# A graph-transformer layer: the feed-forward's first layer and its gelu move behind the summed messages

## The reference

```python
xn = layernorm(x)
# graph attention, 4 heads of 64
h = (xn @ W).reshape(-1, 4, 64)
e = leaky_relu(a_src[src] + a_dst[dst], 0.2)
ex = exp(e - segment_max(e, dst)[dst])
out = segment_sum(ex / segment_sum(ex, dst)[dst] * h[src], dst)
x = x + sigmoid(out + bias) + mixer(xn)
# mixer: softmax of the keys over all nodes, key-value context, queries, a gelu gate, a projection
# feed-forward
y = layernorm(x)
weights = y @ wr + br
chosen = the nodes with the 3124 largest weights
x = x + y, and for the chosen + (gelu(y @ w1 + b1) @ w2 + b2) * weight
```

## Time and profile before

| | |
|---|---|
| median of 3 runs | 1738.97 us |
| profiled execution | 1737.92 us |
| its span, first to last instruction | 1736.1 us |
| TensorE busy | 1156.1 us, 67% |
| VectorE busy | 1040.8 us, 60% |
| GpSimd busy | 853.7 us, 49% |
| ScalarE busy | 568.8 us, 33% |
| mean granted TensorE clock | 0.831 of 2.4 GHz |
| DMA traffic | 212.01 MB, 122 GB/s |

### The profile page before, as it was taken

One profiled execution on the slowest core, in us unless ns is written; L12 is line 12 of the kernel. 1 busy time (PEld: TensorE's weight loads), 2 busy tenths in 40 slices (PEclk: granted clock), 3 DMA queues, 4 the chain that ended last, 5 costly groups with the idle time before them and its releaser, 6 DMA issues. The chain is left out here.

```text
span 1736.1 us, 26200 instructions
## 1 busy us (share of the span) xinstructions
PE 1156.1 (67%) x6583; PEld 864.7 (50%) x6583; DVE 1040.8 (60%) x2649; ACT 568.8 (33%) x1372; POOL 853.7 (49%) x891
## 2 busy tenths in 40 slices
PE   5985546465667777666767686676676766867871
PEld 4653334343455555455555464554555544645651
DVE  6662344446565666666656666576566566666657
ACT  4442222231333333333333333333342333333540
POOL 0703234534566565565655665655556556556000
PEclk9997667777789879898798888988888889788995
DMA  9245154443454454454454544544545444445204
GB/s 255 78 94 123 48 163 117 122 110 101 124 139 132 125 137 122 124 139 120 127 133 120 136 123 125 134 128 125 138 116 137 119 128 130 127 127 138 55 1 148
DMA packets 165872, 212.01 MB, mean 122 GB/s; under 512 B 49492, under 2 KB 131220, under 8 KB 165672
## 3 DMA queue, kind: packets, MB, share of 16 engines
q0 software_dynamic: 39984, 110.94, 25.4%
q1 hardware_dynamic: 117538, 97.15, 19.6%
q10 hardware_dynamic: 8306, 3.41, 0.9%
HBM read 165.93 MB, written 45.46 MB: 122 GB/s over the span
## 5 line engine op out<-in xcount | busy, mean ns | idle before, releaser
L754 POOL DMA_INDIRECT ring<-feat_d,idx x832 | 815.5, 980 | 659.6 <-issue 470.0
L1696 PE MATMUL bank<-ring,hot 128*64 128x265 f32 x1664 | 318.3, 534 | 284.1 <-issue 201.1
L1696 PEld LDWEIGHTS bank<-ring,hot 128*64 128x64 f32 x1664 | 171.8, 190 | 412.3 <-issue 332.4
L1304 DVE TENSOR_TENSOR ring<-ring,bank 128x1024 f32<-128x1024 f32 x208 | 239.8, 1215 | 1.8 <-ACT bank L1491 1.4
L1724 PE MATMUL bank<-late,w_s 128*128 128x128 f32 x1568 | 213.6, 295 | 8.5 <-ACT late L1531 7.8
L1724 PEld LDWEIGHTS bank<-late,w_s 128*128 128x128 f32 x1568 | 207.9, 210 | 14.3 <-ACT late L1531 8.8
L1675 PE MATMUL bank<-w_s,hT 128*128 128x256 f32 x784 | 191.8, 399 | 3.7 <-ACT hT L1538 3.7
L1491 ACT ACTIVATE bank<-diff 128x64 f32<-128x64 f32 x52 | 11.8, 228 | 476.8 <-DVE diff L1291 317.0
L1675 PEld LDWEIGHTS bank<-w_s,hT 128*128 128x128 f32 x784 | 151.2, 199 | 24.3 <-ACT hT L1538 4.3
L1287 DVE TENSOR_TENSOR ring<-bank,lastT 128x64 f32<-128x64 f32 x52 | 11.7, 225 | 236.2 <-remote 210.6
L1538 ACT ACTIVATE hT<-bank,b_s 128x128 f32<-128x128 f32 x392 | 109.3, 376 | 119.1 <-remote 117.7
(11 more groups left out here) (265 smaller groups left out, 1671.3 us busy)
## 6 DMA issues: line engine op xcount, KB each, us to landing
parts_d<-zero SPq DMA_DIRECT2D x59, 265.0 KB
parts_d<-wout SPq DMA_DIRECT2D x208, 66.2 KB
lists<-dloc_d SPq DMA_DIRECT2D x104, 128.0 KB
ring<-feat_d,idx POOLq DMA_INDIRECT x832
parts<-parts_d SPq DMA_DIRECT2D x49, 265.0 KB
xs<-in_x SPq DMA_DIRECT2D x50, 128.0 KB
big<-in_x SPq DMA_DIRECT2D x7, 896.0 KB, 10.8
out<-xnT SPq DMA_DIRECT2D x7, 896.0 KB, 4.2
```

What stands on the lines that cost most here:

```text
L754: pool.indirect_dma_start(out=ring[:, u * TI + q, 0:AW], out_offset=None, in_=feat_d, in_offset=bass.IndirectOffsetOnAxis(ap=idx[:, u, q:q ...
L1304: V.tensor_tensor(feats, feats, ex[:, g * TG:(g + 1) * TG, :].unsqueeze(3) .to_broadcast([P, TG, HEADS, HD]), ALU.mult).then_inc(S("scaled ...
L1696: mm = T.matmul(bank[2 + n][c * WIN:(c + 1) * WIN, 0:SW], hot[:, q, :], ring[:, u * TI + q, 0:SW], start=(j == 0), stop=(j == TG - 1))
```

## The change

On TensorE `first_ff1` and `other_ff1` are taken out of their places behind the turned scores and behind the projection, and put directly before `ff2`, which is behind the sums and `scores_ahead`. On ScalarE `hidden` is taken out of its place before `keep_sums` and put directly before `inverse_root`. Waits and semaphores are the same.

```diff
-steps(act, [EDGES(exps), MERGE(merge_exp), GELU(hidden), EDGES(keep_sums), LOAD_MIXER(load_mixer), MAXIMUM(first_renorm), CONTEXT(context),
-            SUM(inverse_root), MERGE(gates), SUM(keep_turned)])
+steps(act, [EDGES(exps), MERGE(merge_exp), EDGES(keep_sums), LOAD_MIXER(load_mixer), MAXIMUM(first_renorm), CONTEXT(context),
+            GELU(hidden), SUM(inverse_root), MERGE(gates), SUM(keep_turned)])

-steps(pe, [EDGES(turn_scores), FF1(first_ff1), EDGES(turn_maxima), SUM(project), FF1(other_ff1),
+steps(pe, [EDGES(turn_scores), EDGES(turn_maxima), SUM(project),
            EDGES(first_sums), EDGES(other_sums), AHEAD(scores_ahead), MAXIMUM(maximum), CONTEXT(context), PREPARE(prepare),
-           FF1(ff2),
+           FF1(first_ff1), FF1(other_ff1), FF1(ff2),
            FOLD(fold), MERGE(mixer), SUM(turn_normed), SEARCH(search)])
```

## The result

The changed kernel takes 1924.4 us (median of 4 runs, 1920.2 to 1927.6), the kernel before beside it 1737.9 (1731.0 to 1739.7): 1.108 times, interval 1.104 to 1.112, +186.5 us for a forecast of +212.

A forecast was written before the change was run, and what follows sets the result against it. A chain of waits, no full engine, set 26.7 us a step. With sums' end 20.5 us behind the second gather group, +4.7 a step over 45 steps gave +212 on 1737.9: 1950 us, range 1873 to 2030 (8 in 10: 1780 to 2050).

The forecast's parts named there:

- the forecast's own range: Whole kernel: +3 to +6.5 us a step, 1873 to 2030 us, chance 0.62.
- -0.9 from leaky to the sums: Edge scores' end to summed messages' end: 18.4 us, as the second gather group leads leaky by 2.1 instead of 1.3.
- Put onto the chain, +5.5: Behind the sums: scores, both `ff1` halves, last gelus, handovers and a signal start the inverse root 5.5 us later a step.
- term of 0.7 us for one late signal: Behind the moved `ff1`: allowance for TensorE's signal while gathers run, where signals cost from 0.04 to 5.8 us.
- 5.8 us signal: At the moved `ff1`: 5.8 for 0.7 would add 5.1 us more a step and give 2309 us, kept as an end.
- sums' end = second gather group + 20.5 us: Main loop: this distance stays fixed, so the later group makes the next sums end 4.7 us later a step.
- Faster: Turned maxima to VectorE's start: all 5.8 us of late signal go, -1.2 a step, 1684 us; chance 0.09.
- partial relief: Turned maxima to VectorE's start: half of the 5.8 us late signal goes, +1.7 a step, 1815 us; chance 0.21.
- under 17 us: Leaky to the sums: falling below this, with L1287's remote waits mostly gone, would mean relief; under 13.8 the sign is wrong.
- My argument against them: Leaky to sums: the last step, without gathers, had `ff1` in both old places and took 11.8 us, so gathers matter.
- The signs that were named: If right: L1287 every 31 us, second group 10 to 11 behind sums, L1339 waits about 5 longer, leaky to sums 18 to 19.5.
- "`ff1` or its signal too small": ScalarE waiting over 5 us a step for `ff1` (L1724) would show that this cost was set too low.

The follow-up runs named there:

- e4: The changed kernel with its gathers left out from edge block 6 on, GpSimd writing 4 elements a row instead: 1683.3 us.
- e2: The kernel before with only ScalarE's part of the change (gelu behind the copies of the sums): 1941.3 us against 1743.6, 1.114.
- e6: The kernel before with `ff1`'s products cut to 8 streamed columns, all 128 weight columns kept: 1745.1 us against 1737.8, 1.005.
- e12: The kernel before with `ff1`'s products cut to 8 streamed and 32 weight columns: 1744.6 us against 1742.6, 1.000.
- e5: The kernel before with only TensorE's part of the change (both halves of `ff1` behind the sums): 1889.8 us against 1737.8, 1.086.
- e1: The kernel before with the first half of `ff1` moved behind the projection, directly before the second half: 1787.5 us against 1743.6, 1.026.
- e7: Against the kernel before: `ff1` behind the sums, gelu last on ScalarE, `ff2` of the tile before in the hole ahead of the sums: 1772.8 us, 1.022.
- e8: Like e7, but `ff2` stands directly behind `ff1`, the hole is empty and the gelu is last but one: 1826.8 us against 1737.8, 1.050.
- e9: The kernel of e12 (`ff1` cut to 8 streamed and 32 weight columns) on another chip: 1390.0 us against 1387.7 for the kernel before, 1.001.
- e3: The kernel before with its gathers left out from edge block 6 on, GpSimd writing 4 elements a row instead: 1401.7 us against 1743.6.
- e10: The kernel before with `ff1` in 8 products of 256 columns, on another chip: 1389.8 us against 1387.7, 1.000.
- e11: The kernel before with GpSimd's second gather group waiting for `scores_turned` instead of `ff2_done`, on another chip: 1389.5 us against 1387.7, 0.999.

## Why the prediction came out as it did

- **Sign and size.** 1924 lies in the forecast's own range. But the sum held in part by luck, since two terms missed in opposite directions: +9.1 us instead of +5.5 from the sums to leaky, -5.1 instead of -0.9 from leaky to the sums (cut at ScalarE's copy, +6.5 and -2.5: the same signs, smaller misses). Net +4.0 a step where +4.7 was forecast; 45 x 4.0 = 180 of the 186.5 us.
- **Put onto the chain, +5.5.** The instructions were costed rightly: e4 has +4.6 without any late signal, against 4.8, which is the 5.5 without its 0.7 for the signal. What failed is the term of 0.7 us for one late signal, as all that the gathers could cost there: they cost 4.5 us by the shown ends (16.3 - 11.8), and 1.9 by ScalarE's copy. In the step above TensorE's pause ahead of `ff1` costs 2.8 us (ff1 starts 3.1 behind the sums, not 0.3) and the signal 1.7. The range held a 5.8 us signal at this place as an end without a row near it; the truth lay between.
- **The gathers, "sums' end = second gather group + 20.5 us".** This step failed. The distance is 20.4 to 20.9 in the four kernels with TensorE's old order (before, e2, e6, e12), e2 with its group 4.9 us later behind the sums. It is 14.9 in the changed kernel, 15.4 in e5, 17.2 to 22.2 in e1, e7, e8. Two steps of one trace, both of the same order, could not show this. Nor is the distance constant in that trace: over its 41 steps it is 19.3 to 22.1, so 20.5 and 20.4 agreed by chance. In e9, which has the old order on the other chip, it is 11.8.
- **Faster and partial relief.** Their event happened: the 197.5 us at L1287 went, and leaky to the sums is under 17 us (14.3; to ScalarE's copy 17.1). My argument against them (the step without gathers had `ff1` and took 11.8) showed that gathers are needed for the stall, not that it stays when the chain around it is changed. With 5.1 us gone and 5.5 put on, the step would have grown by 0.4 us and the time by about 1%; it grew by 4.0 since the other side grew by 3.6 more. Their reason, `ff1` around the maxima's turn, fails too: e1 makes L1287 early by taking the first half away, but the sums come no earlier; e12 cuts `ff1`'s work and nothing goes; in e8 L1287 is late with no `ff1` near.
- **The signs that were named.** L1287 recurs every 30.6 us, as forecast. The second group starts 15.7 us behind the sums in the mean, not 10 to 11. VectorE waits 11.4 us a step at L1339 for 3.5 before, 7.9 longer and not 5. ScalarE waits 3.0 us a step ahead of its gelus (118.9 us in 40 steps), so the sign for "`ff1` or its signal too small", over 5 us, did not show, though that term was too small: the rest of the stall stands one place earlier, ahead of the copies of the sums.
- **Not costed.** Taking `ff1` out of the hole lowers the clock of the sums. It costs 1.8 us a step without gathers (6.1 for 4.3 us). With gathers it shows no price of its own, since the pauses had lowered the clock before as well: there the sums took 7.2 us at 0.69 in the mean, and take 6.0 at 0.63 in the changed kernel. So a part of what the gathers cost the kernel before is the lower clock that follows a pause.

What stands: the gathers add 7.3 us a step to the kernel before (26.65 - 19.3) and 5.0 to the changed one (30.6 - 25.6). The change costs 6.3 without them, by its chain and the clock of the sums, and gets back 2.3, since the gathers cost it that much less. Cut at ScalarE's copy, the gathers' 7.3 us all lie between leaky and the copy in the kernel before, and 3.1 there and 1.9 behind it in the changed one. **Open:** what makes TensorE stand still. It needs the gathers (e3; their transfers and their issue by GpSimd went together) and does not depend on the size of `ff1`'s products (e12). Gathers alone are not enough, since the same gathers on the other chip bring none. The loading of TensorE's program does not show as a cause either: from 600 to 1600 us of the trace before, where the steps take 26.6 us, only these two queues have packets, and neither is of the kind `instruction`, which the page lists twice for the whole span (packets, MB, share of 16 engines):

```profile
q0 software_dynamic: 28797, 79.91, 31.8%
q1 hardware_dynamic: 59588, 47.93, 16.7%
```

It is not told either whether the changed kernel's order or its 9 us longer chain behind the sums takes most of the stall out of the stretch from leaky to the sums: e1, e7 and e8 changed the order and kept it, e2 made the chain 3.4 us longer and kept it, and no run lengthened the chain by 9 us alone. Whether the number of TensorE's instructions counts was to be told by e10, which ran where the stall is absent and GpSimd sets the pace. What the change costs on that chip was not measured.

## What to carry to other kernels

A constant distance between two events in one trace is a rule only for the order in which it was seen; before it carries a sum, look how far it scatters over all steps, and find one step with another order or shift one side by an experiment. When work is moved behind the point where others wait, add not only its instructions but what the engine that runs it already suffers there: here a signal or a pause of TensorE near gathers cost up to 6 us. And look at which cover the moved work gave: `ff1` in the hole kept the clock up for the sums wherever TensorE did not pause (e3, e10, e11). Before an experiment without effect is read as "this work costs nothing", ask whether another engine sets the pace: in e9 to e11 GpSimd did.

## What the runs showed of the hardware

- The same kernel took 1738 to 1744 us on the chips of most runs and 1388 on one. The transfers were not slower: the gathers' queue was busy for 25.4% of 1736.1 us before and for 31.6% of 1389.9 us in e11, 441 and 439 us of 16 engines. What differs is TensorE: before the maxima's copy VectorE waits 6.0 us in 33 steps of the kernel before, 1.1 us in e11. No trace of the kernel before was taken on that chip; e11 differs from it by one wait of GpSimd. The line of that queue on the page (packets, MB, share of 16 engines), the kernel before:

```profile
q0 software_dynamic: 39984, 110.94, 25.4%
```

and e11:

```profile
q0 software_dynamic: 39984, 110.94, 31.6%
```

- Shown ends of matmuls can lie 6 us ahead of their signals: 819.13 to 824.86 in e1. The Trainium skill (Perfetto Trace Analysis, "Tensor Engine Instruction (MATMUL, LD_WEIGHTS)") calls the shown end an estimate. The rows of e1 agree: TensorE's own next products stop until 824.03, so the time is TensorE's and not the signal's way alone.
- `ff1` ahead of the sums keeps their clock up, on one chip and with the same gathers: with the whole `ff1` there they take 4.2 us at a granted clock of 1.00 (e11), with `ff1` cut down 5.6 us at 0.67 (e9).
- Weight loads set the pace of short products: with 8 streamed columns instead of 128 a product of `ff1` took 323 ns for 295, at a mean granted clock of 0.719 for 0.831 (e6); with 32 weight columns instead of 128 as well it took 194 ns at 0.721 (e12).
